# A two-stage graph network on one core: counting ahead of time, barriers without a drain, another scatter order, edges first in a beat

## The reference

```python
h = relu(layernorm(x))
x = x + segment_sum((h @ W[r])[etypes, src], dst) + h_bias     # 16 relations from 8 bases
h = relu(layernorm(x))
h = leaky(h @ enc_w + enc_b)
for l in range(2):
    agg = segment_sum(h[src], dst) * inv_deg
    h = leaky(agg @ lin_l_w[l] + lin_l_b[l] + h @ lin_r_w[l])
x = x + h                                                      # leaky slope 0.1
```

## Time and profile before

| | us |
|---|---|
| three runs | 3346.27, 3352.03, 3352.49 |
| median | 3352.03 |
| profiled execution | 3354.09 |
| its span | 3352.3 |
| granted TensorE clock, mean | 0.907 |
| PE busy | 2449.3 (73%) |
| DVE busy | 2895.6 (86%) |
| ACT busy | 1926.6 (57%) |
| POOL busy | 2413.4 (72%) |
| DMA | 969.08 MB, mean 289 GB/s |

### The profile page before, as it was taken

One profiled execution on the slowest core, in us unless ns is written; L12 is line 12 of the kernel. 1 busy time (PEld: TensorE's weight loads), 2 busy tenths in 40 slices (PEclk: granted clock), 3 DMA queues, 4 the chain that ended last, 5 costly groups with the idle time before them and its releaser, 6 DMA issues. The chain is left out here.

```text
span 3352.3 us, 50059 instructions
## 1 busy us (share of the span) xinstructions
PE 2449.3 (73%) x13942; PEld 1819.1 (54%) x13942; DVE 2895.6 (86%) x8396; ACT 1926.6 (57%) x4951; POOL 2413.4 (72%) x2412
## 2 busy tenths in 40 slices
PE   2899999999998588888888888477777736663000
PEld 2455555555555466666666666367777735552000
DVE  4899999999998799999999999689889978776567
ACT  0676777677766688888888888445445411110000
POOL 5577777777775577777777777577777757778771
PEclk9999999999999799999999999789999978766555
DMA  9989988986221899999999998389999989999999
GB/s 238 384 311 299 273 260 264 267 261 207 79 86 51 283 284 283 284 285 280 287 284 281 288 286 264 119 288 343 337 327 345 305 311 417 416 415 407 405 403 360
DMA packets 642450, 969.08 MB, mean 289 GB/s; under 512 B 70661, under 2 KB 412295, under 8 KB 630370
## 3 DMA queue, kind: packets, MB, share of 16 engines
q1 hardware_dynamic: 532598, 717.70, 63.6%
q0 software_dynamic: 85376, 194.22, 18.1%
q10 hardware_dynamic: 24198, 53.96, 4.8%
HBM read 509.25 MB, written 464.73 MB: 291 GB/s over the span
## 5 line engine op out<-in xcount | busy, mean ns | idle before, releaser
L981 PE MATMUL y_ps_rel<-w_basis,ht_rel 128*128 128x512 f32 x1568 | 740.2, 595 | 0.0
L712 POOL DMA_INDIRECT agg<-rows_rel,put_c x392 | 387.5, 989 | 165.7 <-issue 97.0
L1260 ACT ACTIVATE h_node<-base_node,shift_node,rstd_node 128x128 f32<-128x128 f32 x1176 | 500.4, 483 | 1.6 <-DVE shift_node L1340 1.6
L1120 POOL DMA_INDIRECT base_and_means<-rows_node,odd_c x392 | 388.2, 990 | 144.1 <-issue 118.0
L1111 POOL DMA_INDIRECT term_node<-agg,src_c x392 | 394.5, 1006 | 131.3 <-issue 119.5
L1800 POOL DMA_INDIRECT gat_l<-base_and_means,src_c x392 | 394.5, 1006 | 119.7 <-issue 119.7
L368 POOL DMA_INDIRECT gat_rel<-in_x_dram,src_c x392 | 384.0, 980 | 131.6 <-issue 103.6
L834 DVE SCALAR_TENSOR_TENSOR two_rel<-y_ps_rel,coef,two_rel 128x128 f32<-128x128 f32 x1568 | 437.6, 341 | 0.0
L981 PEld LDWEIGHTS y_ps_rel<-w_basis,ht_rel 128*128 128x128 f32 x1568 | 269.0, 192 | 189.7 <-issue 149.2
L993 PEld LDWEIGHTS sum_ps_rel<-same_rel,two_rel 128*128 128x128 f32 x1568 | 236.7, 191 | 186.9 <-issue 173.3
L918 ACT ACTIVATE part_rel<-y_ps_rel,coef 128x128 f32<-128x128 f32 x784 | 243.2, 363 | 144.2 <-PE y_ps_rel L981 144.1
(11 more groups left out here) (216 smaller groups left out, 6354.9 us busy)
## 6 DMA issues: line engine op xcount, KB each, us to landing
pairs_l<-base_and_means SPq DMA_DIRECT2D x112, 512.0 KB, 6.6
base_and_means<-zero_row SPq DMA_DIRECT2D x49, 1024.0 KB
means<-zero_row SPq DMA_DIRECT2D x49, 1024.0 KB
first_node<-in_x_dram SPq DMA_DIRECT2D x196, 256.0 KB, 4.0
term_node<-agg SPq DMA_DIRECT2D x196, 256.0 KB, 4.8
x<-base_node SPq DMA_DIRECT2D x196, 256.0 KB, 4.9
base_and_means<-done_node SPq DMA_DIRECT2D x196, 256.0 KB, 4.5
out_dram<-last_z_l SPq DMA_DIRECT2D x98, 512.0 KB, 10.6
```

The costliest lines, as they stand in the source:

```text
L712: nc.gpsimd.indirect_dma_start(agg, bass.IndirectOffsetOnAxis(ap=put_c[:, t:t + 1], axis=0), rows[:, m % KEPT, j, :], None).then_inc(s_sca ...
L981: nc.tensor.matmul(y_ps[(q + j) % 2][:, c * 512:(c + 1) * 512], ht[:, q, j, :], w_basis[:, 4 * c:4 * c + 4, :], start=True, stop=True).the ...
L1120: nc.gpsimd.indirect_dma_start(pair.rearrange("n (k f) -> (n k) f", k=2), bass.IndirectOffsetOnAxis(ap=odd_c[:, t:t + 1], axis=0), rows[:, ...
L1260: last = nc.scalar.activation(h[:, n % 2, j * P:(j + 1) * P], base[:, n % SLOTS, j * P:(j + 1) * P], ACT.Relu, bias=shift[:, b % 2, c:c + ...
```

## The change

Four things are changed.

1. **Counts of half steps.** `need` is no longer computed at the start of the last pass. In the relational pass SP loads, at m = 20, the first destination of every half step into 98 partitions (each partition gets the same 56 numbers of 4 bytes, 3584 bytes apart in DRAM); POOL makes one row number per partition; DVE does four small operations at the start of half step 24 (the comparison is now 98 partitions by 55); SP stores the 98 counts to DRAM at m = 32, and loads them in one row at the start of the last pass, ahead of its loop.
2. **Barriers.** All six Blocks are built with `no_gpsimd_drain=True`, and the barrier in `clear` with `sem_only=True`.
3. **Late scatter.** The first four half steps are scattered in the order 52, 53, 54, 55, then 51, 50 and on down. `s_final` is raised by four when the last of these four has landed, then by one each.
4. **Edges first in a beat.** `is_edges(n)` is n % 3 == 0; `block_of`, the gather's item, the first load of `run_b` and one guard in `to_rows` follow.

```diff
-            with nc.Block() as block:
+            with nc.Block(no_gpsimd_drain=True) as block:
...
-            nc.all_engine_barrier()
+            nc.all_engine_barrier(sem_only=True)
...
+                COUNT_AT, STORE_AT = 24, 32
...
+                        nc.gpsimd.iota(part_i[:], [[0, 1]], base=0, channel_multiplier=LAST).then_inc(s_border, 1)
...
+                            if m == COUNT_AT - 4:
+                                    sp.dma_start(firsts[0:COUNT, :], dst_s.rearrange("(m e) -> m e", e=HALF * P)[:, 0]
+                                                 .partition_broadcast(COUNT)).then_inc(s_firsts, DMA)
+                            if m == STORE_AT:
+                                sp.wait_ge(s_above, 4)
+                                    sp.dma_start(need_d.unsqueeze(1), needed[0:COUNT, :]).then_inc(s_firsts, DMA)
...
+                        sp.wait_ge(s_firsts, 2 * DMA)
...
+                        def count_needed():
+                            dve.wait_ge(s_border, 2)
+                            nc.vector.tensor_scalar(limit[:], part_i[:], float(N - LAST), None, ALU.min).then_inc(s_above, 1)
+                            dve.wait_ge(s_above, 1)
+                            dve.wait_ge(s_firsts, DMA)
+                            nc.vector.tensor_scalar(above[0:COUNT, :], firsts[0:COUNT, 1:HALVES], limit[0:COUNT, :], None,
+                                                    ALU.is_ge).then_inc(s_above, 1)
+                            dve.wait_ge(s_above, 2)
+                            nc.vector.reduce_sum(above_n[0:COUNT, :], above[0:COUNT, :], AX.X).then_inc(s_above, 1)
+                            dve.wait_ge(s_above, 3)
+                            nc.vector.tensor_scalar(needed[0:COUNT, :], above_n[0:COUNT, :], 1.0, None, ALU.add).then_inc(s_above, 1)
...
                         def step(m, q, i):
                             more = before(m, HALVES - 1)
+                            if m == COUNT_AT:
+                                count_needed()
...
                 def is_edges(n):
-                    return n % 3 == 2
+                    return n % 3 == 0
                 def block_of(n):
-                    return n // 3 * 2 + n % 3
+                    return n // 3 * 2 + n % 3 - 1
...
-                            n = 3 * i + 2
+                            n = 3 * i
...
-                            if n >= 20 and valid(n - 12, True):
+                            if n >= 18 and valid(n - 12, True):
...
-                            if 3 * i + 7 > ITEMS + 2:
+                            if 3 * i + 5 > ITEMS + 2:
...
-                    sp.wait_ge(s_need, 1)
+                    sp.wait_ge(s_need, DMA)
...
-                        if l:
-                            nc.gpsimd.iota(limit_i[:], pattern=[[LAST, COUNT]], base=0,
-                                           channel_multiplier=0).then_inc(s_limits, 1)
...
-                        def put_late(m):
-                            q, edges = m % 2, HALVES - 1 - m
+                        def put_late(at, m):
+                            q, edges = at % 2, HALVES - 1 - m
...
-                            if m >= 2:
-                                for j in range(HALF):
-                                    pool.wait_ge(s_late[q][j], use(m - 2, q))
-                                pool.sem_inc(s_final, 1)
+                            if at >= 2:
+                                confirm(at - 2)
...
+                        def confirm(at):
+                            for j in range(HALF):
+                                pool.wait_ge(s_late[at % 2][j], use(at - at % 2, 0))
+                            if at >= FRESH - 1:
+                                pool.sem_inc(s_final, FRESH if at == FRESH - 1 else 1)
...
-                            for m in range(HALVES):
-                                put_late(m)
+                            for at in range(HALVES):
+                                put_late(at, FRESH - 1 - at if at < FRESH else at)
...
+                        sp.dma_start(need[:], need_d.unsqueeze(0)).then_inc(s_need, DMA)
                         steps(sp, load, 2 * span, HALVES - span, HALVES, span)
...
                         select(0, 0)
                         find_open(0, 0)
-                        count_needed(dve)
                         leak(0, 0)
```

More of the change, by code:

```diff
@@ L118, in gnn_kernel @@
         spill = dram("means_by_edge", [HALVES, P, HALF * P])
+        COUNT = -(-N // LAST)
+        assert COUNT <= P
+        need_d = dram("half_steps_needed", [COUNT], I32)
         ident = sb("ident", [P, P])
@@ L654, in relational_pass @@
                 need = buf("need", [1, CHECKS * 2], I32)
+                part_i = buf("part_i", [P, 1], I32)
+                limit = buf("limit", [P, 1])
+                firsts = buf("firsts", [P, HALVES], I32)
+                above = buf("above", [P, HALVES - 1])
+                above_n = buf("above_n", [P, 1])
+                needed = buf("needed", [P, 1], I32)
+                s_firsts, s_above = psem("firsts_loaded_then_needs_stored"), psem("needs_counted")
+                COUNT_AT, STORE_AT = 24, 32
                 s_zeroed = [psem(f"means_zeroed{k}") for k in range(4)]
@@ L754, in _ @@
                             spill(m)
+                            if m == COUNT_AT - 4:
+                                with nc.allow_non_contiguous_dma(reason="the first destination of each half step"):
+                                    sp.dma_start(firsts[0:COUNT, :], dst_s.rearrange("(m e) -> m e", e=HALF * P)[:, 0]
+                                                 .partition_broadcast(COUNT)).then_inc(s_firsts, DMA)
+                            if m == STORE_AT:
+                                sp.wait_ge(s_above, 4)
+                                with nc.allow_non_contiguous_dma(reason="one count of each part"):
+                                    sp.dma_start(need_d.unsqueeze(1), needed[0:COUNT, :]).then_inc(s_firsts, DMA)
                             if m == 0:
@@ L1473, in layer_pass @@
                     pairs = buf("pairs", [P, SWEEP, NB, 2 * P])
-                    KEPT = 8
+                    KEPT, FRESH = 8, 4
                     late = buf("late", [P, 2, HALF, P])
@@ L1623, in layer_pass @@
                     s_both, s_leaky, s_sum = psem("both"), psem("leaky"), psem("sum")
[L1624 to L1627 removed]
                     need = buf("need", [1, COUNT], I32)
[L1629 to L1630 removed]
+                    s_final, s_need = psem("half_steps_added"), psem("need_loaded")
                 def part(ap, k):
                     return ap[bass.ds(first_row(k), LAST), :].rearrange("(p j) f -> p (j f)", p=P)
[L1636 to L1652 removed]
                 def loaded(k):
@@ L1838, in _ @@
                                 back(KEPT + m)
-                            for m in range(HALVES):
-                                put_late(m)
-                            for q in range(2):
-                                for j in range(HALF):
-                                    pool.wait_ge(s_late[q][j], DMA * HALVES // 2)
-                                pool.sem_inc(s_final, 1)
+                            for at in range(HALVES):
+                                put_late(at, FRESH - 1 - at if at < FRESH else at)
+                            for at in (HALVES - 2, HALVES - 1):
+                                confirm(at)
                     @block.sync
```

22 lines of the change are left out of this document (removed).

## The result

| | before | after |
|---|---|---|
| median of 13 runs each, us | 3351.44 | 3341.64 |
| lowest, highest | 3346.27, 3360.62 | 3338.94, 3351.04 |
| profiled execution, span | 3354.09, 3352.3 | 3338.94, 3337.2 |
| granted TensorE clock | 0.907 | 0.91 |
| stages by the Block ends: relational | 83.1 to 1101.3 | 78.9 to 1089.5 |

The ratio is 0.9972, 95% interval 0.9962 to 0.9982: 9.4 us less (6 to 13), against 29.7 forecast, and 1.6 above the upper end of the range. The joined pass, which should have become 7.3 us shorter (6.6 and 4.0 off, 3.3 on), has become 10.9 longer.

The account below looks back on a forecast made before the run. Each stage has its own limit (relational PE and DVE busy, joined DVE, write-out DMA), so gains lie at borders. 4.0 + 9.2 + 6.8 + 8.8 − 0.7 − 3.3 + 4.0 + 0.9 = 29.7; median 3322.3, range 3308 to 3340.

Parts of the forecast that it names:

- In between, DVE's work for a beat is the same, so the beat stays: Joined pass, edges first: between its start and end the beat was to stay at 10.38 us.
- Rival 3: Joined pass: uneven leaks make each beat 0.7 us longer, 69 us in all, median 3391; chance 0.07.
- 9.2 forecast: Border from relational stage to joined pass: dropping POOL's DRAIN of 9298 ns gains 9.2 us.
- 6.8 forecast: Border from joined to last pass: DRAIN 6.6 and second barrier about 0.2, together 6.8 us gained.
- Rival 1: Borders: drain work cannot be left out; gain 13.9, median 3338.1, or 3342.1 without the setup's 4.0; chance 0.10.
- the setup's 4.0: Border from setup to relational stage: without POOL's DRAIN the stage starts 4.0 us earlier; other end 0.
- 8.8 forecast: Start of last pass: moving the counts out lets gathers and first leak start earlier, 8.8 us gained, high end 10.6.
- Rival 2: Start of last pass: the 9.58 us gather stays, counts bring about 0.2 us, median 3330.9; chance 0.06.
- rival 4: Relational stage: loading 5488 small pieces holds SP's queue; 3372 at 64 us, near 3337 at 30; chance 0.05.
- The 0.7 for DVE: Relational stage: four added small DVE operations cost 0.7 us, charged in full; other end 0.
- Forecast 3.3 and −4.0: Joined pass, edges first: its start costs 3.3 us, its end gains 4.0 (0 to 6.9).
- 0.9 forecast: Late scatter order: 3.2 us gained by work moved forward, first means 2.3 later, net gain 0.9 (−4 to +10).

Follow-up runs that it names:

- e2: Kernel before with only the edges put first in a beat; 3366.54 us, ratio 1.0045.
- e3: Changed kernel with the edges last in a beat again, all else as changed; 3327.94 us, ratio to before 0.9932.
- e4: Changed kernel with find_open moved right behind select, edges still first; 3326.39 us, ratio to before 0.9925.
- e7: Changed kernel without the joined pass's scatters and the waits for them; single execution, first to last add 1007.8 us.
- e8: Changed kernel with find_open moved ahead of the leak in its own step; single execution, 3327.58 us.
- e1: Kernel before with only the barriers changed (six Blocks and the barrier in clear); 3341.94 us, ratio 0.9967.
- e5: Kernel before with only the counts of half steps moved into the relational pass; 3339.03 us, ratio 0.9966.
- e9: e1 with the last pass's leak split in two, its add one carry earlier; 3368.42 us, ratio to before 1.0044.
- e10: Kernel before with the last pass's leak split in two, its add one carry earlier; 3384.6 us, ratio 1.0095.
- e13 to e18: Barriers again: e1 twice, before with drains removed at single borders (two variants), e4 with drains back twice; 4125.81 to 4197.17 us, before 4161.3 and 4185.16.
- e6: Kernel before with only the new order of the late scatter; 3351.4 us, ratio 0.9999.
- e11: The kernel of e4 run once more, unchanged; 3324.09 us.

## Why the prediction was wrong

**The beat.** The step that failed is "In between, DVE's work for a beat is the same, so the beat stays". The same operations do not take the same time: find_open takes 0.42 or 0.63 us, by what POOL does in that moment, and with DVE busy all the time the difference is the beat's. It cost 16.8 us from first to last add (14.5 in e2, alone), and it is gone in e3, e4, e7 and e8. Rival 3 named the place (the beat of the joined pass, from 0.30 us a beat on it would decide the sign), with 0.07 too low a chance, and gave it the wrong mechanism and price: uneven leaks and 0.7 a beat; it was 0.17, too little to turn the sign. I took DVE's durations from a beat of before and moved them about as if they were constants. The row that spoke against this was used elsewhere in the same text: the gather of 9.58 us, which shows that DVE and POOL hold each other up. And the trace of before has the long find_open itself, at 1126.18. The Trainium skill (SBUF — State Buffer, "Who interferes with whom") has the rule that I did not weigh: tensor_scalar can run in a mode that takes both port pairs, and then contends with GpSimd. The timelines agree in part: find_open is a tensor_scalar with one source in SBUF, and where it stood elsewhere beside POOL, or had no scatter for a neighbour (e3, e4, e7, e8), it took 0.42. But it also took 0.42 when it lay wholly inside a scatter (1501.83 to 1502.25, in one from 1501.52 to 1502.49), so to run beside POOL is not enough, and in which mode it ran no trace says.

**The barriers.** The two large terms at the borders were right: 9.2 forecast, and between the start of the last scatter and the Block's end 12.0 us before and 2.6 after, so 9.4; 6.8 forecast, and from POOL's last landing to its first gather of the last pass 8.8 us before and 2.3 in e1, so 6.5. Rival 1 falls with e1: the DRAINs are gone, and at each Block's end the other engines go on within 0.3 us of POOL. That the measured 3341.64 is 0.5 us from its second price, 3342.1, is chance. Its argument that the DRAINs are longer than any landing also fails for the one of 6575 ns: scatters of the write-out (L1805) take up to 8.2 us to land. Of the setup's 4.0 only 1.9 arrived, and the wait that took over is ACT's for the first run_b, before and after:

```profile
86.60 1.04 ACT L910 ACTIVATE open_rel<-run_b_rel,ones 128x896 f32<-128x896 uint8 x1 [12.89 <-DMA run_b_rel<-run_in_tile]
```

```profile
84.73 1.04 ACT L946 ACTIVATE open_rel<-run_b_rel,ones 128x896 f32<-128x896 uint8 x1 [12.97 <-DMA run_b_rel<-run_in_tile]
```

It ends 1.9 us earlier, though the stage starts 4.2 earlier. Between 80 and 85 us the DMA share is 0.62 before and 1.00 after, so the load probably stands behind the setup's own gathers now; no run separates them. I had bounded this term at 0 but named no next wait. In the total the barriers are worth 9 to 11 us by e1, 11 by e3 against e5 (3339.03 − 3327.94, on two chips, with the scatter order in it), and 16 by e9 against e10, where 20.0 were forecast. What failed here is to add the three border terms up as a gain of the whole: 18 us are shown at the borders, and e1 keeps 9 to 11 of them. In its profiled execution 5.5 of the 7.9 us that the loop of the last pass is longer are POOL's, in gathers that take longer. Whether that follows from the missing drains or differs from execution to execution is open; e13 to e18 could not decide it.

**The counts.** 8.8 forecast; the first leak came 8.8 sooner, and e5 shows 11.4 (8 to 15). The sum took the right lower value: POOL's gather was the limit, and it was held up by the comparison on DVE. (The "8.3 us earlier" of its working is 8.6, 2175.2 − 2165.33 − 1.27; it changes nothing.) Rival 2, the long gather stays, falls, and with it, for this kernel, the inference of the Trainium skill's section named there that a tensor_tensor does not hold up software descriptors. The long gather is in every trace that has the comparison (e1 9.58, e2 10.32, e6 9.56) and in none without it. The load of 5488 small pieces took SP 429 ns:

```profile
L769 SPq DMA_DIRECT2D firsts_rel<-dst_sorted x1: 429/429/429, 408.3 to 408.3; - x1
```

My bounds of 10 and 64 us were both far off, and rival 4 falls. How long the load held up later ones is not in that row, but e5 as a whole leaves no room for 50 us. The 0.7 for DVE was not paid either: the relational stage took 1010.4 us in e1, without the four operations, and 1010.6 in the changed kernel.

**Edges first, start and end.** Forecast 3.3 and −4.0. In the profile the first small operation is at 1105.09, 15.6 after the Block's end, before 11.7: 3.9.

```profile
1100.46 0.69 DVE L1345 TENSOR_TENSOR base_node<-first_node,term_node 128x512 f32<-128x512 f32 x1 [10.57 <-DMA term_node<-agg,src_c]
...
1105.09 0.18 DVE L1358 TENSOR_TENSOR apart_node<-st_node 128x12 f32<-128x12 f32 x1
```

The end: from the last add to POOL's last landing 32.9 us before (2117.0 to 2149.9), 28.9 after (2126.5 to 2155.4): 4.0.

**The scatter order.** 0.9 forecast, 0 measured (−3 to +4), which does not tell the two apart. Its two parts were each mis-sized: 3.2 for the work that moves forward is 5.0, and 2.3 for the later start is 3.7 (e6) to 4.9 in the changed kernel, and 8.8 in e11, where the leaks end sooner but POOL's 28 scatters don't.

**The sum.** In the two profiled executions: borders and relational stage −11.8 (forecast −12.5); joined pass with its border +10.9 (−7.3); last pass −14.2 (−9.9), of which −8.8 at its start, −5.5 in the loop, +4.9 and −4.8 for the order. The 5.5 are hardly more than e4 and e11 differ by; yet with the leak whole, the seven traces with the counts moved lie at 497.6 to 506.4 and the four without at 502.9 to 514.6, so a part of it may belong to the counts. By the single parts over many runs: −11 (barriers), −11.4 (counts), 0 (order), +15 (edges first), together some −7.5 beside the measured −9.4. So the loss of the whole, 20.3 us beside the forecast, is nearly all in two places: 15 to 17 us in the beat, and 9 of the barriers' 20.0, with some 3 more than forecast from the counts against them. (The range's lower end has a slip, too: all high ends together are 17.8 more gain, not "some 14". The miss was at the upper end.)

**Better than both** is e4: the change as it is, with find_open behind select, 3326.39 us (0.9925 of before). e3, with the edges last, is as good within the spread, 3327.94; so edges first bring nothing of their own that can be measured here (their start and end were forecast at 3.3 and −4.0 and measured at 3.9 and −4.0).

## What to carry to other kernels

Where DVE and POOL are both busy without a pause, a DVE operation's duration can depend on its place in time, and so can that of a DMA that POOL issues: after a reordering compare the duration of each operation of both engines, line by line, before looking for waits or at the clock, and try its few possible places. A removed stall at a border is worth what the next stage can do with it: look for what the first operation behind it waits for (here a load, with the DMA share at 1.00). And take the spread of executions apart by stage before an effect of a few us is believed or explained.

## What was not expected of the hardware

- DVE and POOL fall into step: with no wait for a semaphore in the steady beats, both have a period of 10.42 us, and after the reordering both 10.59, at a fixed offset over at least 20 beats.
- A comparison of 512 elements takes 0.42 us when it starts 0.12 before or 0.31 after a scatter's start, or 0.81 into a gather, and 0.60 to 0.67 when it starts 0.53 to 0.59 us into a scatter (188 times) or a gather (twice).
- Moving one of two neighbouring DVE operations ahead by one carry in the last pass made POOL's 392 gathers 33 us longer in sum (385.40 to 418.55), with POOL waiting for nothing in either kernel.
- 5488 pieces of 4 bytes in one load cost SP 429 ns of issue; the zero fills of 1 MB with 2048 pieces cost 3.8 us. The count of pieces does not give the time of issue.
- The granted clock of the last pass's loop, with the leak whole, is 0.95 to 0.98 from kernel to kernel and from execution to execution, and the loop's length goes with it, 514.6 to 497.6 us.
